# A first pass that loads two tiles in one transfer of 16896 bytes per partition, into four double buffers

## The chip, the cores and the metric

The kernel runs on one core of a Trainium2 chip. The metric is device microseconds of one execution. An engine is named as in the profile: PE is the matrix engine (PEld its weight loads), DVE the vector engine, ACT the scalar engine, POOL GpSimd, SP the engine that issues most transfers. SPq and ACTq are the instruction queues of SP and ACT, in which transfers (DMA) are issued.

## The reference

The input is x, 16 channels of 2048 x 2048 float32 (268 MB). Four layers follow one another, each `x = x + conv(gn(x))`:

```python
def _gn(v, G=8, eps=1e-5):            # mean and variance over 2 channels x 2048 x 2048
    return ((g - m) / jnp.sqrt(s + eps)).reshape(v.shape)
# conv: the 15 ways to partition {row in, column in, row out, column out};
# each is an einsum of X (itself, its transpose, its diagonal, its row, column and total
# sums, spread over rows, columns, the diagonal or everything) with a 16x16 weight
for i, blocks in enumerate(PARTITIONS):
    Yi = _basis_apply(X, weights[i], blocks, eye_n, ones_n)   # divided by N per summed index
    Y = Yi if Y is None else Y + Yi
return Y + jnp.sum(bias)
```

All of this is linear apart from the normalisation, which needs only a mean and a variance per pair of channels. So the kernel reads x twice: once for its statistics (row sums, column sums, a Gram matrix of the channels, the diagonal), from which small algebra gives one 32x32 channel mixing matrix with its row and column terms for all four layers together, and once to apply them and write the result.

## The kernel before

**First pass, lines 322 to 330, 447 to 452, 456 to 460, 510 to 518 and 661 to 686.** The host lays x out as 272 tiles (`pair_tiles`, `lay_out`): 64 rows by 128 columns of x and of its transpose, 32 channels in all, as 128 partitions of `VW` = 2112 floats, that is 8448 bytes. They lie one after another in DRAM, so that a tile is one contiguous block of 1056 KB. On the chip the tensor `early` holds `V_SLOTS` = 8 such tiles, side by side on each partition; tile t goes to slot t mod 8.

SP runs the loop over the tiles. It issues the first 8 loads at once; after the eighth (t == 7) come the constants and two copies of the diagonal. Before tile t from the ninth on it waits until PE and DVE have finished tile t - 8 (`gram_done` and `summed`, one count per tile). Each slot has its own semaphore `v_in`, which a load raises by 16 as it lands.

For each tile DVE makes one reduction (line 515), the column sums, which POOL adds to `col_sum` (line 449). PE makes 32 matmuls (line 668; the trace counts 64 records for them), which add four tiles, a quad, into four PSUM banks; two quads use the banks in turn, and after each ACT copies them out (line 460) and POOL adds the copy to the Gram matrix and the row sums (lines 365 and 368; in POOL's order, the sum of a quad comes after the column sums of the next one). After tile 4, DVE waits for the constants and the diagonal before it goes on (lines 519 to 523), and PE has a small product of the diagonal between the second and the third quad. PE's quads from the third on are a loop, in which quad q waits until quad q - 2 has been copied out.

**Between the passes.** Once the last tile is in the sums, DVE (lines 540 to 626), PE (691 to 746) and ACT work through the algebra of the four layers in turn, one waiting for the other at nearly every step. SP has by then issued the loads of the first units of the second pass: six and a half units go to `ring_own`, a tensor of their own (lines 333 and 334), and three into `early`, once PE and DVE have finished all tiles (lines 335 to 345); one more may go into `early` only after the algebra.

**Second pass.** x is 256 strips of 128 partitions x 2048 floats and a half strip; two strips are a unit, loaded in one transfer of 2048 KB, 16384 bytes on each partition (line 317), and stored in one (line 494, issued by ACT). PE multiplies each strip by the mixing matrix (line 763), DVE adds the row and column terms back into the buffer (lines 639 and 647). A buffer is loaded again once its store has landed.

Of the kernel before, what the change touches and what calls it, by code (L numbers as in the profile page):

```python
# [8 lines left out]
BLK = 128  # L9
# [11 lines left out]
VW = RANGE // SUB * FOUR  # L21
QUAD = 4
V_SLOTS = 2 * QUAD
# [10 lines left out]
def pair_tiles(n):  # L34


    nb = n // BLK
    out = []
    for J in range(nb // 2 + 1):
        for e in range(2):  # L40
            for first in (J, nb - J) if 0 < J < nb // 2 else (J,):
                out += [(2 * first + e, k) for k in range(first, nb)]
    return out


def quads(n):

    tiles = pair_tiles(n)
    return [list(dict.fromkeys(r for r, _ in tiles[t:t + QUAD])) for t in range(0, len(tiles), QUAD)]


def strips(n):


    groups = n // SUB
    out = [[(0, 0, 0, n)]]
    for q in range(1, groups // 2):
        out.append([(0, q, SUB * q, n - SUB * q), (n - SUB * q, groups - q, n - SUB * q, SUB * q)])
    return out + [[(0, groups // 2, n // 2, n // 2)]]


def lay_out(x):

    n = x.shape[2]
    x = x[0]
    xt = np.ascontiguousarray(x.transpose(0, 2, 1))
    tiles = pair_tiles(n)
    v = np.zeros((len(tiles), BLK, RANGE // SUB, FOUR), np.float32)
    row, col = np.arange(RANGE)[:, None], np.arange(BLK)[None]
    for t, (r, J) in enumerate(tiles):  # L70
        at = PAIR * SUB + COLS * quads(n)[t // QUAD].index(r)
        v[t, :, :, at:at + COLS] = 1.0
        rows, cols = slice(r * RANGE, (r + 1) * RANGE), slice(J * BLK, (J + 1) * BLK)
        for h, a in enumerate((x, xt)):
            blk = a[:, rows, cols]
            if r * RANGE // BLK == J:
                i, j = row + r * RANGE, col + J * BLK
                blk = np.where((i <= j if h == 0 else i < j)[None], blk, np.float32(0))
            blk = blk.reshape(CH, RANGE // SUB, SUB, BLK).transpose(3, 1, 0, 2)
            v[t, :, :, h * CH * SUB:(h + 1) * CH * SUB] = blk.reshape(BLK, RANGE // SUB, CH * SUB)  # L80
    z = np.zeros((len(strips(n)), 2, CH, SUB, n), np.float32)
    for q, strip in enumerate(strips(n)):
        for at, g, j, width in strip:
            for h, a in enumerate((x, xt)):
                z[q, h, :, :, at:at + width] = a[:, SUB * g:SUB * g + SUB, j:j + width]
    return v.reshape(len(tiles), BLK, VW), *as_units(z.reshape(len(strips(n)), BLK, n))


def as_units(z):

    count, _, n = z.shape
    twos = z[:count - 1].reshape(count // 2, 2, BLK, n).transpose(0, 2, 1, 3)
    return np.ascontiguousarray(twos).reshape(count // 2, BLK, 2 * n), np.ascontiguousarray(z[count - 1, :, 0:n // 2])
# [80 lines left out]
def build(nc, n, v, twos, half, dia, dia_pair, weights, biases, const_f32, twos_out, half_out, out_dia, where):  # L174
# [6 lines left out]
    tiles = pair_tiles(n)  # L181
# [11 lines left out]
    with ctx:  # L193
        def sb(name, shape, dt=F32):
            return ctx.enter_context(nc.sbuf_tensor(name, shape, dt))

        def sem(name):
            return ctx.enter_context(nc.semaphore(name))

        Z_OWN = 13  # L200
        early = sb("early", [BLK, V_SLOTS * VW])
        ring_own = sb("ring_own", [BLK, Z_OWN, n])
        vbuf = early[:, :].rearrange("p (s w) -> p s w", s=V_SLOTS)
# [89 lines left out]
            rows = vbuf[:, s].rearrange("p (q e b) -> p q e b", q=RANGE // SUB, b=COLS)  # L293
            return rows[:, k // COLS, 0:width, k % COLS]

        v_in = [sem(f"v_in{s}") for s in range(V_SLOTS)]
        z_in = [sem(f"z_in{s}") for s in range(TWOS + 1)]
        z_out = [sem(f"z_out{s}") for s in range(TWOS + 1)]
        const_in, dia_loaded, weights_in = sem("const_in"), sem("dia_loaded"), sem("weights_in")
# [1 line left out]
        gram_done, summed, sum_added = sem("gram_done"), sem("summed"), sem("sum_added")  # L301
# [11 lines left out]
        @block.sync  # L313
        def _(sp):
            def load(u):
                buf, s, _ = home(u)
                sp.dma_start(buf, half if s == TWOS else twos[units[u][0] // 2]).then_inc(z_in[s], 16)  # L317

            for layer in range(LAYERS):
                sp.dma_start(wt[:, layer], weights[layer].rearrange("k c o -> c k o")).then_inc(weights_in, 16)  # L320
                sp.dma_start(bias_sb[:, layer], biases[layer].rearrange("(z k) -> z k", z=1)).then_inc(weights_in, 16)
            for t in range(len(tiles)):
                if t >= V_SLOTS:
                    sp.wait_ge(gram_done, t - V_SLOTS + 1)
                    sp.wait_ge(summed, t - V_SLOTS + 1)
                sp.dma_start(vbuf[:, t % V_SLOTS], v[t]).then_inc(v_in[t % V_SLOTS], 16)
                if t == V_SLOTS - 1:
                    sp.dma_start(const[:, :], const_f32).then_inc(const_in, 16)
                    sp.dma_start(dia2[:, :, :], dia_pair).then_inc(dia_loaded, 16)
                    sp.dma_start(dia_in[:, :, :], dia).then_inc(dia_loaded, 16)  # L330
            sp.wait_ge(matrices_in, 16 * 13)
            sp.wait_ge(dia_cov_done, 1)
            for u in range(own_twos + 1):
                load(u)
            sp.wait_ge(gram_done, len(tiles))
            sp.wait_ge(summed, len(tiles))
            for u in range(own_twos + 1, len(units)):
                _, s, turn = home(u)
                if turn == 0 and s >= own_twos + reuse:
                    sp.wait_ge(col_term_done, 1)  # L340
                    sp.wait_ge(row_term_done, 1)
                    sp.wait_ge(dia_ready, 1)
                if turn:
                    sp.wait_ge(z_out[s], 16 * turn)
                load(u)
            for s in range(TWOS):
                sp.wait_ge(z_out[s], 16 * len(range(s, half_strip // 2, TWOS)))
            sp.wait_ge(z_out[TWOS], 16)
            sp.wait_ge(dia_out, 16 * 4)
# [151 lines left out]
        def _(dve):  # L501
# [7 lines left out]
            tt = nc.vector.tensor_tensor  # L509
            for t in range(len(tiles)):  # L510
                s = t % V_SLOTS
                dve.wait_ge(v_in[s], 16 * (t // V_SLOTS + 1))
                if t >= sums:
                    dve.wait_ge(sum_added, t - sums + 1)
                nc.vector.tensor_reduce(  # L515
                    part_sum[:, t % sums],
                    vbuf[:, s].rearrange("p (q w) -> p q w", w=FOUR)[:, :, 0:PAIR * SUB].rearrange(
                        "p q (c a) -> p c q a", a=SUB), AX.XY, ALU.add).then_inc(summed, 1)
                if t == 4:
                    dve.wait_ge(const_in, 16)  # L520
                    dve.wait_ge(dia_loaded, 32)
                    tt(dia2s[:, :, :], dia2[:, :, :], c("dia_scale").unsqueeze(1).to_broadcast([BLK, nb, FEATS]),
                       ALU.mult).then_inc(dia_scaled, 1)
                if t == 8:
                    dve.wait_ge(weights_in, 16 * 2 * LAYERS)
                    link(nc.vector.tensor_reduce(beta[:, :], bias_sb[:, :, :], AX.X, ALU.add))
                    link(nc.vector.memset(brow[:, :, :], 0.0))
                    nc.vector.tensor_copy(brow[:, :, 0:4 * CH],
                                          beta[:, :].unsqueeze(2).to_broadcast([1, LAYERS, 4 * CH])).then_inc(beta_done, 1)
                    link(nc.vector.memset(rs[:, :, :], 0.0))  # L530
                    link(nc.vector.memset(normed[:, :], 0.0))
                    nc.vector.memset(normed[96:97, FEATS:FEATS + 1], 1.0)
                    nc.vector.memset(m80[:, :, :], 0.0)
                    link(nc.vector.memset(mean_row[:, :], 0.0))
# [125 lines left out]
        def _(pe):  # L660
            mm = nc.tensor.matmul
            def quad(parity, turn):
                for slot in range(QUAD * parity, QUAD * parity + QUAD):
                    opens, closes = slot % QUAD == 0, slot % QUAD == QUAD - 1
                    pe.wait_ge(v_in[slot], 16 * (turn + 1))
                    for k in range(CHUNKS):
                        m, lane = k // COLS, k % COLS * WIDE
                        last = mm(regions(parity)[lane:lane + WIDE, m // BANK_REGIONS, m % BANK_REGIONS],  # L668
                                  chunk(slot, k, WIDE), chunk(slot, k, WIDE + MARKS),
                                  start=opens and m % BANK_REGIONS == 0,  # L670
                                  stop=closes and m % BANK_REGIONS == BANK_REGIONS - 1)
                    last.then_inc(gram_done, 1)
# [75 lines left out]
            for p, (u, k, q) in enumerate(order):  # L748
                buf, first = strip_buf(u, k), 4 * (p % 2)
                _, s, turn = home(u)  # L750
# [58 lines left out]
```

## Time and profile before

| | us |
|---|---|
| median of 3 runs | 2044.98 (2041.34 to 2045.75) |
| the profiled execution, its time | 2041.38 |
| its span, first to last instruction | 2039.1 |
| PE / DVE / POOL / ACT busy | 1630.1 / 1333.5 / 256.5 / 79.1 |
| moved by DMA | 834.80 MB in 78957 packets, 409 GB/s over the span |
| first pass: the last tile's load issued, and landed | at 695.92, 18.1 later |
| second pass: first matmul with the mixer | at 805.8 |

Times within the trace are microseconds from the start of the span. Views of the trace that are used below: the 40 equal slices of the span (a digit is a busy share in tenths, PEclk the clock granted to PE); the chain of waits that ended last; the waits by engine; busy times, granted clock, DMA share and GB/s of a stretch; the instructions in order of time; and the time from a transfer's issue to its landing.

### The profile page before, as it was taken

To read this page: it belongs to the slowest core of one execution; us is meant where nothing else is said; L and a number is where in the kernel's file an instruction comes from. 1 tells how busy PE (TensorE), PEld (TensorE's weight loads), DVE (VectorE), ACT (ScalarE), POOL (GpSimd) and SP (SyncE) were. 2 spreads that over 40 slices of the span, in tenths; PEclk is the share of its full clock that TensorE was granted. 3 is DMA by queue.
4 is the path that set the end of the run, shared out by engine and by line. 5 is a ranking of instruction groups with operands and counts; after the bars stand their busy time and mean duration, and the time that the engine had idled before them with its cause. 6 is when DMAs were issued, how large, how long until landed. Compare 5 with 4: busy or idle time off the path is not lost.

```text
span 2039.1 us, 43249 instructions
## 1 busy us (share of the span) xinstructions
PE 1630.1 (80%) x19730; PEld 999.9 (49%) x19730; DVE 1333.5 (65%) x1285; ACT 79.1 (4%) x80; POOL 256.5 (13%) x488
## 2 busy tenths in 40 slices
PE   6888888888888858999887778777877777778773
PEld 6877777777777753344333333333333333333331
DVE  5988888888888832677555555555555555555553
ACT  0111111001111100000000000000000000000000
POOL 6333333333333310000000000000000000000000
PEclk9999999999999965999999999999999999999987
DMA  9999999999999980899999999999999999999998
GB/s 376 416 415 414 422 422 423 422 422 422 422 422 422 424 352 0 331 431 431 430 431 431 431 431 431 431 431 431 431 431 430 431 431 430 431 431 431 431 430 372
DMA packets 78957, 834.80 MB, mean 409 GB/s; under 512 B 10617, under 2 KB 10745, under 8 KB 11321
## 3 DMA queue, kind: packets, MB, share of 16 engines
q1 hardware_dynamic: 59208, 564.76, 65.9%
q10 hardware_dynamic: 19696, 269.40, 30.9%
q8 instruction: 27, 0.44, 0.1%
q14 instruction: 26, 0.20, 0.0%
HBM read 564.73 MB, written 269.09 MB: 409 GB/s over the span
## 4 chain that ended last, share of the span: by engine, by line
another core or an unknown queue 47%; DMA 33%; PE 10%; DVE 6%; SPq 2%; issue 1%; POOL 0%; ACT 0%; DVEq 0%; POOLq 0%
DMA early<-pairs 28%; PE ps L763 6%; DVE ring_own L515 5%; DMA out<-early 2%; SPq L317 2%; DMA early<-strip_in 1%; DMA dia_in<-dia 1%; PE ps L742 0%; PE ps L744 0%; PE ps L738 0%; PE ps L698 0%; PE ps L692 0%; PE ps L770 0%; POOL gram_all L365 0%
## 5 line engine op out<-in xcount | busy, mean ns | idle before, releaser
L763 PE MATMUL ps<-ring_own,mixer 128*128 128x512 f32 x1252 | 592.9, 631 | 137.5 <-DMA ring_own<-strip_in 126.8
L668 PE MATMUL ps<-early 128*64 128x66 f32 x17408 | 590.6, 224 | 121.6 <-DMA early<-pairs 114.3
L515 DVE TENSOR_REDUCE ring_own<-early 128x32 f32<-128x2048 f32 x272 | 619.9, 2285 | 84.0 <-DMA early<-pairs 83.6
L668 PEld LDWEIGHTS ps<-early 128*64 128x64 f32 x17408 | 554.6, 138 | 157.4 <-DMA early<-pairs 130.3
L639 DVE SCALAR_TENSOR_TENSOR ring_own<-ps,row_sum,stage 128x512 f32<-128x512 f32 (+3 forms) x233 | 301.6, 1295 | 331.4 <-PE ps L763 331.4
L763 PEld LDWEIGHTS ps<-ring_own,mixer 128*128 128x128 f32 x1252 | 247.0, 202 | 484.6 <-issue 468.9
L763 PE MATMUL ps<-early,mixer 128*128 128x512 f32 x800 | 374.5, 625 | 89.6 <-DMA early<-strip_in 79.0
L639 DVE SCALAR_TENSOR_TENSOR early<-ps,row_sum,stage 128x1024 f32<-128x1024 f32 (+2 forms) x152 | 192.6, 1267 | 197.2 <-PE ps L763 197.2
L763 PEld LDWEIGHTS ps<-early,mixer 128*128 128x128 f32 x800 | 156.2, 200 | 307.5 <-issue 296.1
L365 POOL TENSOR_TENSOR gram_all<-gram_all,stage 128x1024 f32<-128x1024 f32 x68 | 150.5, 2213 | 0.3
L647 DVE SCALAR_TENSOR_TENSOR ring_own<-ps,row_sum,stage 128x488 f32<-128x488 f32 (+43 forms) x308 | 133.4, 475 | 0.0
L449 POOL TENSOR_TENSOR col_sum<-col_sum,ring_own 128x32 f32<-128x32 f32 x272 | 68.8, 253 | 457.3 <-DVE ring_own L515 456.6
L460 ACT ACTIVATE stage<-ps 128x1056 f32<-128x1056 f32 x68 | 71.7, 1054 | 640.4 <-PE ps L668 640.4
L647 DVE SCALAR_TENSOR_TENSOR early<-ps,row_sum,stage 128x464 f32<-128x464 f32 (+49 forms) x200 | 86.6, 475 | 0.0
L368 POOL TENSOR_TENSOR row_sum<-row_sum,stage 128x16 f32<-128x16 f32 x80 | 18.0, 232 | 0.0
L381 POOL TENSOR_TENSOR ring_own<-ring_own 16x64 f32<-16x64 f32 x51 | 17.2, 338 | 4.0
L692 PE MATMUL ps<-const,early 128*128 128x32 f32 x32 | 7.0, 401 | 7.9 <-DVE early L540 7.9
L692 PEld LDWEIGHTS ps<-const,early 128*128 128x128 f32 x32 | 6.9, 332 | 8.0 <-issue 8.0
L742 PE MATMUL ps<-early,coef_t 80*128 80x512 f32 x8 | 8.3, 1142 | 0.0
L744 PE MATMUL ps<-gram_all 1*128 1x512 f32 x8 | 8.3, 1136 | 0.0
L738 PE MATMUL ps<-early,stage 80*128 80x512 f32 x8 | 7.5, 1099 | 0.8 <-DVE mixer L621 0.8
L722 PE MATMUL ps<-normed,step_m 96*96 96x80 f32 x8 | 2.4, 408 | 7.2 <-DVE normed L598 7.2
(137 smaller groups left out, 133.9 us busy)
## 6 DMA issues: line engine op xcount, KB each, us to landing
early<-pairs SPq DMA_DIRECT2D x272, 1056.0 KB, 18.1
ring_own<-strip_in SPq DMA_DIRECT2D x78, 2048.0 KB, 23.3
out<-ring_own ACTq DMA_DIRECT2D x78, 2048.0 KB, 63.1
early<-strip_in SPq DMA_DIRECT2D x50, 2048.0 KB, 23.3
out<-early ACTq DMA_DIRECT2D x50, 2048.0 KB, 63.4
const<-const_f SPq DMA_DIRECT2D x1, 781.0 KB, 22.2
ring_own<-dia_pair SPq DMA_DIRECT2D x1, 640.0 KB, 21.8
ring_own<-half_in SPq DMA_DIRECT2D x1, 512.0 KB, 36.5
```

What stands on the lines that cost most here:

```text
L317: sp.dma_start(buf, half if s == TWOS else twos[units[u][0] // 2]).then_inc(z_in[s], 16)
L365: nc.gpsimd.tensor_tensor(gram_all[:, :, 0:WIDE], gram_all[:, :, 0:WIDE], got[:, :, 0:WIDE], ALU.add)
L368: last = nc.gpsimd.tensor_tensor(rows, rows, got[:, :, WIDE + k], ALU.add)
L381: link(nc.gpsimd.tensor_tensor(dst, a, b, op))
L449: nc.gpsimd.tensor_tensor(col_sum[:, J], col_sum[:, J], part_sum[:, t % sums], ALU.add).then_inc(sum_added, 1)
L460: nc.scalar.activation(stage[:, q % 2].rearrange("p (b m) w -> p b m w", m=BANK_REGIONS), regions(q), ACT.Copy).then_inc(gram_staged, 1)
L515: nc.vector.tensor_reduce(part_sum[:, t % sums], vbuf[:, s].rearrange("p (q w) -> p q w", w=FOUR)[:, :, 0:PAIR * SUB].rearrange("p q (c a) ...
L639: ins = nc.vector.scalar_tensor_tensor(buf[:, at + done:at + done + wide * BANK].rearrange("p (b w) -> p b w", b=wide), acc[:, b:b + wide] ...
L647: ins = nc.vector.scalar_tensor_tensor(buf[:, at + done:at + done + piece], acc[:, b, off:off + piece], row_term[:, g:g + 1], col_term[:, ...
L668: last = mm(regions(parity)[lane:lane + WIDE, m // BANK_REGIONS, m % BANK_REGIONS], chunk(slot, k, WIDE), chunk(slot, k, WIDE + MARKS), st ...
L692: last = mm(ps[:, 0, b * PAIR:(b + 1) * PAIR], spread[:, b * per_block:(b + 1) * per_block].rearrange("p g a -> p (g a)"), c("pair"), star ...
L763: last = mm(ps[:, first + at // BANK, 0:piece], mixer[:, :, :].rearrange("p c a -> p (c a)"), buf[:, at:at + piece], start=True, stop=True)
```

## The change

The host puts the tiles t and t + 1 (t even) side by side on each partition: 136 blocks of 128 x 16896 bytes in place of 272 of 128 x 8448. SP issues one transfer for two tiles, into two neighbouring slots, and before the fifth and each later one it waits until PE and DVE have finished both tiles that lie there. Four semaphores, one for a pair of slots, stand in place of eight. DVE still waits before each tile, on the semaphore of the pair; PE waits only before the first tile of a pair. The constants are issued after the fourth double transfer, so behind the same 8 tiles. Nothing changes in what DVE, PE, ACT and POOL compute, in which order, or in the second pass. The bytes are the same.

```diff
-    return v.reshape(len(tiles), BLK, VW), *as_units(z.reshape(len(strips(n)), BLK, n))
+    v = v.reshape(len(tiles) // 2, 2, BLK, VW).transpose(0, 2, 1, 3)
+    return np.ascontiguousarray(v).reshape(len(tiles) // 2, BLK, 2 * VW), *as_units(z.reshape(len(strips(n)), BLK, n))
...
-        v_in = [sem(f"v_in{s}") for s in range(V_SLOTS)]
+        v_in = [sem(f"v_in{s}") for s in range(V_SLOTS // 2)]
...
-            for t in range(len(tiles)):
+            for t in range(0, len(tiles), 2):
+                s = t % V_SLOTS
                 if t >= V_SLOTS:
-                    sp.wait_ge(gram_done, t - V_SLOTS + 1)
-                    sp.wait_ge(summed, t - V_SLOTS + 1)
-                sp.dma_start(vbuf[:, t % V_SLOTS], v[t]).then_inc(v_in[t % V_SLOTS], 16)
-                if t == V_SLOTS - 1:
+                    sp.wait_ge(gram_done, t - V_SLOTS + 2)
+                    sp.wait_ge(summed, t - V_SLOTS + 2)
+                sp.dma_start(early[:, s * VW:(s + 2) * VW], v[t // 2]).then_inc(v_in[s // 2], 16)
+                if t == V_SLOTS - 2:
...
-                dve.wait_ge(v_in[s], 16 * (t // V_SLOTS + 1))
+                dve.wait_ge(v_in[s // 2], 16 * (t // V_SLOTS + 1))
...
-                    pe.wait_ge(v_in[slot], 16 * (turn + 1))
+                    if slot % 2 == 0:
+                        pe.wait_ge(v_in[slot // 2], 16 * (turn + 1))
```

## Rows read from the trace of the kernel before

**Rows 1.** The span in 40 slices: granted PE clock, mean share of 16 DMA engines.

```profile
PEclk9999999999999965999999999999999999999987
DMA  9999999999999980899999999999999999999998
```

**Rows 2.** Waits: engine, line, what it waited for: total us, times, longest.

```profile
PE ps L668 <- DMA early<-pairs: 114.3, 253, 8.8
...
DVE ring_own L515 <- DMA early<-pairs: 83.6, 248, 8.8
...
SPq L325 <- DVE ring_own L515: 578.0, 264, 12.6
```

**Rows 3.** DMA queues: packets, MB, share; issues: count, KB each, us to landing.

```profile
q1 hardware_dynamic: 59208, 564.76, 65.9%
q10 hardware_dynamic: 19696, 269.40, 30.9%
...
early<-pairs SPq DMA_DIRECT2D x272, 1056.0 KB, 18.1
```

**Rows 4.** Stretches: busy PE, PEld, DVE, ACT, POOL (count), clock, DMA share, GB/s.

```profile
200.00:712.00 512.00, 430.72 (x12736) 403.33 (x12731) 454.67 (x200) 52.69 (x50) 167.90 (x309) 1.00 1.01 422
45.00:50.00 5.00, 3.25 (x105) 3.11 (x101) 5.00 (x3) 1.05 (x1) 0.51 (x2) 1.00 1.00 414
50.00:55.00 5.00, 4.70 (x102) 4.70 (x104) 5.00 (x3) 0.00 (x0) 2.81 (x4) 0.66 1.01 421
1000.00:1900.00 900.00, 703.36 (x1477) 290.83 (x1476) 492.24 (x655) 0.00 (x0) 0.00 (x0) 0.94 1.01 431
```

**Rows 5.** The chain of waits, in order of time: start, us, what.

```profile
199.06 18.09 DMA early<-pairs
...
363.41 18.78 DMA early<-pairs
...
693.35 18.11 DMA early<-pairs
...
1107.28 9.44 another core or an unknown queue
...
1909.80 9.42 another core or an unknown queue
```

**Rows 6.** First-pass loads (line 326): all 272, to landing.

```profile
DMA to landing us min/median/max: 5.1/18.1/22.7
```

**Rows 7.** SP's queue after the last tile; the last strip load, to landing.

```profile
695.92 0.33 SPq L326 DMA_DIRECT2D early<-pairs  x1
...
L317 SPq DMA_DIRECT2D early<-strip_in x1: 434/434/434, 717.3 to 717.3; - x1
...
DMA to landing us min/median/max: 42.1/42.1/42.1
```

**Rows 8.** Instructions in order of time: start, us, engine, line, what, [idle before].

```profile
32.03 1.49 DVE L522 TENSOR_TENSOR ring_own<-ring_own,const 128x1280 f32<-128x1280 f32 x1 [9.30 <-DMA dia_in<-dia]
...
44.14 41.76 DVE L515 TENSOR_REDUCE ring_own<-early 128x32 f32<-128x2048 f32 x19
...
44.08 4.17 PE L668 MATMUL ps<-early 128*64 128x66 f32 x128 [1.31 <-issue]
50.30 5.67 PE L668 MATMUL ps<-early 128*64 128x66 f32 x128 [2.05 <-issue]
```

**Rows 9.** The same, from the last tile to the first step of the algebra.

```profile
714.05 2.29 DVE L515 TENSOR_REDUCE ring_own<-early 128x32 f32<-128x2048 f32 x1 [0.28 <-DMA early<-pairs]
...
714.07 2.19 PE L668 MATMUL ps<-early 128*64 128x66 f32 x64 [0.40 <-DMA early<-pairs]
...
716.41 0.25 POOL L449 TENSOR_TENSOR col_sum<-col_sum,ring_own 128x32 f32<-128x32 f32 x1 [2.31 <-DVE ring_own L515]
...
721.67 2.29 DVE L540 TENSOR_TENSOR early<-row_sum,const 128x2048 f32<-128x2048 f32 x1 [5.34 <-POOL row_sum L368]
```

## The prediction

> **What bounds the kernel now.** I read the slices of the whole span first [rows 1]. DMA shows a 9 in every slice but three in the middle and the last: in both passes the 16 DMA engines are full nearly everywhere, and only the algebra between the passes leaves them idle. The stretch from 200 to 712 says the same more closely [rows 4]: DMA share 1.01 (the view counts about half a per cent too much), while PE is busy 430.7 of 512 us and DVE 454.7. The waits come next [rows 2]: both PE and DVE wait for tiles to land, some 250 times, about 0.4 us each on average, so they are faster than the transfers. SP's long wait for DVE (578.0 us) looks like the bound and isn't one: it is the wait for a free slot. What decides is how much work lies in the queue when SP is let go. A lone first tile lands 5.1 us after its issue, the usual one after 18.1 [rows 6], so the usual tile stands behind seven others (7 x 2.57 = 18.0).
>
> Next I take rates from distances between equal events, which the windows blur. In the chain of waits a load that was 8 tiles further on starts at 199.06 and 24 rows later at 693.35, one row per 8 tiles [rows 5]: 494.29 / 192 = 2.574 us per tile of 1.0813 MB, 420.0 GB/s. In the second pass (82 units from 1107.28 to 1909.80 [rows 5]) a unit takes 9.787 us for a load and a store of 2.097 MB each: 428.6 GB/s. Strips alone, without stores: the last tile lands at 695.92 + 18.1 = 714.0, the last of nine and a quarter strip loads behind it at 717.3 + 42.1 = 759.4 [rows 7], so 45.4 / 9.25 = 4.908 us each, 427.3 GB/s. Rows of 16384 bytes move 1.7 to 2.0% faster than rows of 8448, with stores or without.
>
> **How much of that is packets.** The packet counts settle what a row is [rows 3]. The ACT queue has 19696: 128 stores x (128 rows + 16) = 18432, and the small ones give the rest. So a row of 16384 bytes is one packet, and each DMA adds one short packet per engine, its semaphore. SP's queue: 272 x 144 = 39168 for the tiles and 20040 for the others, 59208. Every DMA, tile or strip, is thus 8 rows and one short packet on each engine. Taking time per DMA = a + bytes per engine x b: tile 67584 B in 2.574 us, strip unit 131072 B in 4.908. b = 2.334 / 63488 = 36.8 ns per KB of 1000 bytes, a = 2.574 - 2.484 = 0.090 us, about 10 ns per packet.
>
> **The change, part by part.**
>
> 1. Loads. 136 DMAs of 8 x 16896 bytes per engine: 0.090 + 135168 B x 36.76 ns/KB = 5.059 us, against 2 x 2.5744 = 5.149. Saved, a once for each pair, 0.090 x 136 = 12.2 us, all on the path, because DMA is full from the first tile to the last (a byte that comes earlier brings all later ones forward). The packets fall by 136 x 144 = 19584, to 59373 in all. Ends for this term: with the second pass's unit in place of the lone strips (9.787 / 2 = 4.893) a is 0.106 and the saving 14.4 us. Without the irregular tiles (one chain row in six is 18.78 in place of 18.1 [rows 5]; a tile without them is 2.562) a is 0.065 and the saving 8.8. Outer ends: nothing, if the row is not what costs; and 24.5 us, if a vanishes at 16896 bytes (135168 B alone are 4.969 us). I take 12.2, the value from loads without stores.
>
> 2. The first pass's end. The last two tiles now land together. Before, DVE started the last tile at 714.05 and the algebra followed from there: reduction 2.29, then POOL's sums, then line 540 at 721.67 [rows 9]. Now DVE has two reductions after the landing, and the first costs 2.20 when it follows without a gap (41.76 / 19 [rows 8]): +2.2 us. PE's 2 x 2.19 ends sooner than DVE's 4.5, and ACT's copy lies beside POOL's work. Nothing hides this: in the algebra DMA runs dry in any case (the 0 in [rows 1]), and the second pass starts when the algebra ends. The algebra itself is unchanged, its PE at the low clock as before.
>
> 3. Waits and issues. SP issues 136 fewer DMAs at 0.33 us each [rows 7]; SP is never late, so nothing. PE loses 136 waits on semaphores that are up: nothing; ends -0.1 and 0.
>
> 4. Depth of the buffers: what the coarser release costs. Slots come free in twos, 4.5 us after a landing. At that moment the next pair has 0.5 us to go and two stand behind it: 10.6 us of queued transfers. Before it was 18.1 - 2.57 = 15.5. What must be covered is a lone load's overhead, 5.1 - 2.57 = 2.5 us. It is covered four times over, so 0 us; landing should take 4 x 5.059 - 4.6 = 15.6 us in place of 18.1. The thinnest place is the start. DVE stands until 32.03 for the diagonal [rows 8], so the slots of tiles 4 and 5 come free together at about 35.7. Behind the constants, which land as DVE resumes, there are then tiles 8 to 11, good until 32 + 10.1 = 42.1. Tiles 6 and 7 free theirs at 40.1, 8 and 9 (with DVE's extra work after tile 8, about 1.9 us before 44.14) at 46.4, when the queue reaches to 52. At least 5 us are left, more later. If that cover were gone, each such release would cost what it is late, 2 to 3 us once or twice.
>
> Sum: 2041.38 - 12.2 + 2.2 = 2031.4 us for an execution like the profiled one (span 2029.1). That execution is 3.6 below the median of the runs shown (2044.98), near their lowest; the same difference on the median gives 2035.0. Between the two I say 2033.0.
>
> **A rule weighed against the trace.** The Trainium skill (page "DMA: Bandwidth & Descriptors", section "Bandwidth", under why small descriptors are slow) says that a packet costs a fixed 3 cycles or so beside one beat per 32 bytes. With the beat at 32 x 36.76 / 1000 = 1.18 ns that is 3.5 ns where the rows give 10; by it the change would save 1224 packets per engine x 3.5 ns = 4.3 us, 2.1 after the tail. The same page's section "Rules for kernel authors" asks for 1 MiB per DMA for full bandwidth, which a tile already is; it speaks against any gain. The rows speak for one, since strips of 2 MiB do go faster.
>
> **Rivals.**
>
> A. The row isn't what costs. Tiles and strips could differ for another reason, such as instruction fetches or the irregular 18.78 landings, which would stay; or a packet costs a third of what I give it. Saving 0 to 4.3, tail +2.2: time 2039.3 to 2043.6, no change that can be told. For it: the irregular landings alone account for 0.5 of the 2%. Against it: two independent strip rates agree. The same end comes if a row above 16384 bytes, which no DMA here has, is cut into 16384 + 512: packets fall only by the semaphores' 136 x 16 (to 76781), the saving is 136 x 10 ns, and the time 2042.2.
>
> B. Slower: PE falls to 1.2 GHz inside the first pass. Two tiles in a row are 4.3 us of matmuls, and the gap grows from 0.4 to 5.06 - 4.3 = 0.75 us. At the low clock a pair takes 8.6 us of PE, more than the 5.06 of its transfer, and its release would come later than the 10.6 us queue less the 2.5 can bear for long: 3.6 us lost for every such pair. It cancels the gain from 3 pairs (10.0 / 3.6) and shows as slower from 4 (14.1 / 3.6), some 35 us at the low clock beyond what the queue absorbs. If 10% of the pass were so, 8 pairs, +28 us: 2060. For it: after an idle PE of 2.05 us at 50.30 the clock shows 0.66 [rows 4, 8], and the second pass, with its longer gaps, has 0.94. Against it: an idle of 1.31 us (44.08) left it at 1.00 [rows 4, 8], and 0.75 is shorter. The start may have one dip more (PE waits for the diagonal after tile 7), which ends within a few us, and the queue holds 5.
>
> C. More than forecast: the fixed part shrinks with the longer row, or 8448-byte rows suffer otherwise. Up to 24.5 saved less 2.2: 2019.1.
>
> **Numbers.** Forecast 0.71, with its own range 2028 to 2038; A 0.15; B 0.07; C 0.07. Less than 0.2% (4.1 us) is about what a measurement of this kernel can't tell from no change. Faster: forecast and C, with a rounding down for the spread of the runs, 0.77. Same: A, 0.15. Slower: B and an unforeseen loss in the transfers, 0.08. The range reaches to C's middle and A's end, 2024 to 2045.
>
> **What the profile after would show.** Right: 136 first-pass loads of 2112 KB, about 59370 packets, 15 to 16 us to landing; equal marks in the chain 20.2 us apart for 8 tiles where they were 20.5 to 20.6; the stretch 200 to 700 at 429 to 431 GB/s by the window view, which gave 422; the last pair landing near 701.8; line 540 at 711.7 (9.9 after that landing, where it was 7.7). Then all as before, 10.0 earlier. Wrong: some 76800 packets; the rate at 422 (A); a PEclk below 9 in the first pass's slices beyond 50 us, or a DMA digit below 9 there (B); a landing under 12 us, which would mean that the queue runs nearly dry.

## The result, and the profile after

| | before | after |
|---|---|---|
| median us | 2044.98 (2041.34 to 2045.89, 7 runs) | 2037.58 (2034.81 to 2038.35, 7 runs) |
| ratio | | 0.9966, 95% interval 0.9954 to 0.9977 |
| profiled execution: time, span | 2041.38, 2039.1 | 2037.44, 2035.2 |
| packets | 78957 | 59370 |
| last landing of the first pass | 714.0 | 704.4 |
| first step of the algebra (line 540, now 542) | 721.67 | 714.25 |
| from there to the end of the span | 1317.4 | 1321.0 |

The change makes the kernel faster by 7.4 us (0.34%). The forecast was 2033.0, with its own range of 2028 to 2038; the time lies 4.6 us above the forecast and 0.4 us inside the range.

Slices of the span after, the SP queue's packets, the loads, and the stretch from 200 to 700, which answer to [rows 1, 3, 4]:

```profile
PEclk9999999999999955899999999999999989999997
DMA  9999999999999960899999999999999999999998
...
q1 hardware_dynamic: 39624, 564.75, 65.4%
...
early<-pairs SPq DMA_DIRECT2D x136, 2112.0 KB, 15.6
...
200.00:700.00 500.00, 405.47 (x12639) 392.23 (x12636) 442.33 (x199) 52.56 (x50) 168.15 (x307) 1.00 1.01 428
```

The rate rose from 422 to 428 in the view's counting (forecast 429 to 431), landing takes 15.6 us as worked out, PE's clock is 1.00 in this stretch and the packets are 59370. The chain of waits gives the exact distances. Two neighbouring rows of before, each 8 tiles behind the last:

```profile
281.41 18.11 DMA early<-pairs
301.90 18.13 DMA early<-pairs
```

and after, as [rows 5]:

```profile
202.81 15.64 DMA early<-pairs
...
283.58 15.59 DMA early<-pairs
...
303.75 15.60 DMA early<-pairs
...
688.80 15.61 DMA early<-pairs
```

A mark is the distance between two such rows, 8 tiles. From 202.81 to 688.80 are 24 marks, 20.25 us each with the irregular ones (forecast 20.24), where they were 20.60. An undisturbed mark is 20.17 to 20.20, where it was 20.5. The end of the pass, as [rows 9] (start, us, engine, line):

```profile
704.44 4.48 DVE L517 TENSOR_REDUCE ring_own<-early 128x32 f32<-128x2048 f32 x2 [0.57 <-DMA early<-pairs]
...
714.25 2.29 DVE L542 TENSOR_TENSOR early<-row_sum,const 128x2048 f32<-128x2048 f32 x1 [5.33 <-POOL row_sum L370]
```

Both tiles of the last pair are reduced after one landing, and the algebra starts 9.8 us behind it (forecast 9.9; before, 7.6 from 714.05 to 721.67). The landing was forecast near 701.8 and the algebra at 711.7; both came 2.6 us later.

The last row of the table is a trap. The two spans differ by 3.9 us, the medians by 7.4. The part behind the first pass has two lengths that come whatever the kernel: 1317.4 in the profile of before, 1317.9 in one variant below (e_two_rows), and 1320.1 to 1321.6 in ten profiles, those of four kernels with rows of 8448 bytes or fewer among them. The profile of before was a short one, that of after a long one. Line 540 against line 542 shows the change itself: 7.4 us, as do the medians.

### The profile page after: what moved, and what is told of

It reads as the page before. It is cut to its first block, busy times and chain, and to the rows that moved or that the text cites. A ratio compares the mean times of both kernels' runs of the same rounds, so it can differ in the third digit from the quotient of the medians.

```text
span 2035.2 us, 42981 instructions
## 1 busy us (share of the span) xinstructions
PE 1607.9 (79%) x19730; PEld 990.7 (49%) x19730; DVE 1322.1 (65%) x1285; ACT 78.9 (4%) x80; POOL 258.7 (13%) x488
## 2 busy tenths in 40 slices
DMA packets 59370, 834.78 MB, mean 410 GB/s; under 512 B 8440, under 2 KB 8568, under 8 KB 9144
## 3 DMA queue, kind: packets, MB, share of 16 engines
q1 hardware_dynamic: 39624, 564.75, 65.4%
## 4 chain that ended last, share of the span: by engine, by line
another core or an unknown queue 47%; DMA 28%; PE 12%; DVE 5%; issue 4%; SPq 2%; POOL 0%; ACT 0%; DVEq 0%; POOLq 0%
DMA early<-pairs 24%; PE ps L766 6%; DVE ring_own L517 4%; PE ps L671 3%; DMA out<-ring_own 2%; SPq L318 2%; DMA early<-strip_in 1%; PE ps L745 0%; PE ps L747 0%; PE ps L741 0%; PE ps L701 0%; PE ps L695 0%; PE ps L773 0%; PE ps L772 0%
## 5 line engine op out<-in xcount | busy, mean ns | idle before, releaser
L671 PE MATMUL ps<-early 128*64 128x66 f32 x17408 | 560.1, 223 | 146.0 <-DMA early<-pairs 129.2
L517 DVE TENSOR_REDUCE ring_own<-early 128x32 f32<-128x2048 f32 x272 | 608.5, 2281 | 90.5 <-DMA early<-pairs 90.4
L671 PEld LDWEIGHTS ps<-early 128*64 128x64 f32 x17408 | 542.5, 138 | 163.5 <-DMA early<-pairs 112.6
L766 PE MATMUL ps<-early,mixer 128*128 128x512 f32 x800 | 379.3, 631 | 88.4 <-DMA early<-strip_in 66.9
## 6 DMA issues: line engine op xcount, KB each, us to landing
early<-pairs SPq DMA_DIRECT2D x136, 2112.0 KB, 15.6
```

The costliest lines, as they stand in the source:

```text
L517: nc.vector.tensor_reduce(part_sum[:, t % sums], vbuf[:, s].rearrange("p (q w) -> p q w", w=FOUR)[:, :, 0:PAIR * SUB].rearrange("p q (c a) ...
L766: last = mm(ps[:, first + at // BANK, 0:piece], mixer[:, :, :].rearrange("p c a -> p (c a)"), buf[:, at:at + piece], start=True, stop=True)
```

## Experiments

All are compared by the median, and by two places in the trace: the distance of undisturbed marks, and the start of the algebra. Each ratio is to the kernel before as it ran beside that kernel, with medians of 2043.32 to 2045.05; so medians of different rows can be off by a microsecond or two against each other. The algebra's start of one profile isn't exact either: three profiles of the same schedule and packets (changed, c_after, x_after_shift) have 714.25, 714.52 and 715.94.

| kernel | bytes of a packet | DMAs of the pass | mark | algebra at | median (runs) | ratio to before, 95% |
|---|---|---|---|---|---|---|
| before | 8448 | 272 | 20.5 | 721.67 | 2044.98 (7) | |
| changed | 16896 | 136 | 20.2 | 714.25 | 2037.58 (7) | 0.9954 to 0.9977 |
| c_after | 16896 | 136 | 20.2 | 714.52 | 2036.83 (5) | 0.9950 to 0.9977 |
| x_src | 8448 | 272 | 20.5 | 721.17 | 2044.19 (11) | 0.9986 to 1.0004 |
| x_after_shift | 16896 | 136 | 20.2 | 715.94 | 2037.58 (5) | 0.9946 to 0.9974 |
| e_half_rows | 4224 | 272 | 20.5 | 721.68 | 2043.85 (10) | 0.9987 to 1.0006 |
| e_two_rows | 8448 | 136 | 20.5 | 723.66 | 2046.74 (11) | 1.0000 to 1.0018 |
| e_gap2 | 8448 | 136 | 20.5 | 724.08 | 2046.34 (10) | 1.0002 to 1.0021 |
| e_gap4 | 4224 | 136 | 20.5 | 723.54 | 2047.03 (8) | 1.0005 to 1.0025 |
| e_mat_a | 16896 | 136 | 20.2 | 712.78 | 2036.05 (5) | 0.9940 to 0.9967 |
| e_last_single | 16896 | 137 | 20.2 | 718.90 | 2038.67 (10) | 0.9964 to 0.9983 |
| e_combo | 16896 | 136 | 20.2 | 710.99 | 2033.70 (5) | 0.9940 to 0.9967 |
| e_quads | 33792 | 68 | 22.5 (mean) | 796.59 | 2121.85 (2) | 1.0357 to 1.0395 |

**The changed kernel again** (c_after, no edit).

> The changed kernel again, for a second profile of it. Theory 1 (the gain is made in the first pass and nothing in the second pass depends on the change): the first step of the algebra starts 7.4 us earlier than in the kernel before's profile (714.25 against 721.67), within 0.3, and what lies between that and the end differs from profile to profile by some 3 us either way; the median is 7 to 8 us below the kernel before. Theory 2 (the change also makes the second pass slower, as the first pair of profiles has it: gain 7.4 at the algebra, 3.9 at the end): the end is again only about 4 us earlier than 2039.1.

Algebra at 714.52, rest 1321.2, median 7.6 below the kernel before that ran beside it. Theory 1 stands: a second pass of the changed kernel isn't slower; kernels with the old rows (x_src 1321.3, e_half_rows 1321.5) have the long rest too.

**What of a transfer is cheaper: the DMA, the packet, or its place?** First the changed kernel's schedule with the rows of before (e_two_rows):

```diff
-    v = v.reshape(len(tiles) // 2, 2, BLK, VW).transpose(0, 2, 1, 3)
-    return np.ascontiguousarray(v).reshape(len(tiles) // 2, BLK, 2 * VW), *as_units(z.reshape(len(strips(n)), BLK, n))
+    return v.reshape(len(tiles) // 2, 2, BLK, VW), *as_units(z.reshape(len(strips(n)), BLK, n))
...
-                sp.dma_start(early[:, s * VW:(s + 2) * VW], v[t // 2]).then_inc(v_in[s // 2], 16)
+                sp.dma_start(vbuf[:, s:s + 2], v[t // 2].rearrange("s p w -> p s w")).then_inc(v_in[s // 2], 16)
```

> The changed kernel's schedule (136 DMAs, release and semaphore by pairs), but each partition's 16896 bytes come as two rows of 8448, as the tiles lay before. Packets per pair and engine: 17, where the changed kernel has 9 and the kernel before 18. Theory P (each packet costs about 10 ns): the rate stays at 420 GB/s, saving 136 x 10 ns = 1.4 us, tail +2.2, so about 1 us slower than the kernel before (2046) and 8 slower than the changed one. Theory D (the cost is one of the DMA or its semaphore, not of the rows): as the changed kernel, 2037.6, marks 20.18 us apart for 8 tiles.

The gain is gone (an undisturbed mark is 20.5 again) and the tail stays, 2046.74: the number of DMAs and semaphores is not what costs. Then the kernel before with rows cut in two (e_half_rows: v laid out as two planes of 128 x 1056 floats per tile, loaded by `v[t].rearrange("h p w -> p h w")`):

> The kernel before with each tile's rows cut in two, 4224 bytes each: 272 DMAs as before, 17 packets per engine and DMA in place of 9. Theory P: 272 x 8 x 10 ns = 21.8 us slower than before, 2066.8, marks 20.5 + 0.64 = 21.1 us apart. Theory D: no change, 2045. In between, the cost per packet can be read off: excess / 2176.

This one went against me. There are 34816 more packets and no more time. So a fixed 10 ns for each packet, my model, is wrong, although it had given the right rate for 16896 bytes. Two more kernels ask whether the start of a row decides: x_src lays the rows of before 8704 bytes apart in DRAM, so that each starts at a multiple of 512, and x_after_shift lets the changed kernel's start 256 bytes past a multiple of 512 on both sides (`early[:, 64 + s * VW:64 + (s + 2) * VW]` from `v[t // 2][:, 64:64 + 2 * VW]`).

> The kernel before, its rows of 8448 bytes laid 8704 apart in DRAM, so that every row starts at a multiple of 512 bytes there (before, every second one starts 256 past one). SBUF side, row length, DMAs and packets unchanged. Theory A (half of the 8448-byte rows pay for their start in DRAM): marks of 8 tiles fall from 20.50 towards 20.18, time 2035 to 2040. Theory L (the length of the row, or what is left of it over whole blocks of 512, is what counts) and theory S (the start in SBUF counts): no change, 2044.

> The changed kernel with its rows of 16896 bytes starting 256 bytes past a multiple of 512, in DRAM (rows 17408 apart) and in SBUF. Theories A and S: each row now pays as the misaligned ones before, marks 20.18 rise to about 20.3 to 20.5, time 2040 to 2044. Theory L: no change, 2037.

Neither moves: marks 20.5 and 20.2, medians as their parents'. The start is out. (That x_after_shift's algebra starts 1.4 to 1.7 us behind the other two comes from the first 90 us, point 4 below, and from a few more irregular marks, not from the pace.) The last pair keeps everything of the changed kernel but the packet, by a gap of 256 bytes in DRAM after every k-th part of a row (k = 2, and 4 in e_gap4):

```diff
-    return np.ascontiguousarray(v).reshape(len(tiles) // 2, BLK, 2 * VW), *as_units(z.reshape(len(strips(n)), BLK, n))
+    pieces = np.zeros((len(tiles) // 2, BLK, 2, 2112 + 64), np.float32)
+    pieces[:, :, :, 0:2112] = v.reshape(len(tiles) // 2, BLK, 2, 2112)
+    return pieces, *as_units(z.reshape(len(strips(n)), BLK, n))
...
-                sp.dma_start(early[:, s * VW:(s + 2) * VW], v[t // 2]).then_inc(v_in[s // 2], 16)
+                sp.dma_start(early[:, s * VW:(s + 2) * VW].rearrange("p (k w) -> p k w", k=2),
+                             v[t // 2][:, :, 0:2112]).then_inc(v_in[s // 2], 16)
```

> The changed kernel, but a partition's 16896 bytes lie in DRAM as two pieces of 8448 with a gap of 256 bytes, so that a packet carries 8448 bytes while the place in DRAM, the destination, the order and the number of DMAs stay. Packets of a pair: 17 per engine in place of 9. Theory B (what counts is how many bytes one packet moves): as the kernel before, marks of 8 tiles 20.5 apart (two pieces a megabyte apart gave that), time 2045 to 2047 with the tail. Theory N (what counts is that the two tiles are neighbours in DRAM): as the changed kernel, 20.18 and 2037.

> The same with four pieces of 4224 bytes and gaps of 256: 33 packets per pair and engine. A fixed cost of about 9 ns per packet would give 8 x 9 x 4 x 2 = 0.6 us more per mark than two pieces, 21.1, and 2060. Rows of 4224 bytes in an order of their own gave 20.51 instead; if that holds, the gain from 4224 to 8448 is nil and only the step to 16896 pays: marks 20.5, time 2046.

Queue and chain of e_gap2:

```profile
q1 hardware_dynamic: 57032, 564.75, 65.8%
...
657.38 15.90 DMA early<-pairs
...
677.85 15.91 DMA early<-pairs
...
698.34 15.90 DMA early<-pairs
```

and of e_gap4:

```profile
q1 hardware_dynamic: 91848, 564.75, 66.2%
...
656.80 15.91 DMA early<-pairs
...
677.28 15.93 DMA early<-pairs
...
697.79 15.92 DMA early<-pairs
```

20.47 and 20.49 us per mark with 57032 packets, 20.48 and 20.51 with 91848, 20.2 with 39624. What the gain needs is packets of 16896 bytes; between 4224 and 8448 the shorter packet costs nothing more. Why the step lies there no run shows, nor whether the strips with their 16384 bytes owe their rate to the same.

**Where the missing gain went** (e_mat_a). The chain fixes the pair of tiles 78 and 79: before it was complete at 219.74, in the changed kernel at 218.47, in its second profile at 217.94. That is 1.3 and 1.8 us of gain for 40 pairs, where 3.6 were due; the other 96 pairs brought 8.3 and 7.5 (8.6 due). In that time ACT issues 12 small transfers of the layer matrices, 4 rows of 384 bytes for each of 16 partitions; 10 of them fall between 88 and 194 us. One line makes them rows of 1536:

```diff
-        place = [place_buf[:, m * wsize:(m + 1) * wsize].rearrange("p (l r o) -> p l r o", l=LAYERS, r=6)
+        place = [place_buf[:, m * wsize:(m + 1) * wsize].rearrange("p (r l o) -> p l r o", l=LAYERS, r=6)
```

> The changed kernel with the layer matrices laid out on GpSimd's side so that each of the 12 small transfers between quads 5 and 16 has one row of 1536 bytes per partition in place of four of 384. In that stretch the profiles give 10.5 us for two pairs against 10.12 elsewhere, 0.37 per small transfer (0.25 in the kernel before). Theory M (their short packets cost it): 3 to 3.5 us less from 88 to 193 us, the 24th to 34th landing at the steady pace, time 2034. Rival (the cost is per small DMA or comes from GpSimd, DVE or ACT): under 1 us, 2037.

Two equal places 40 tiles apart (DVE, in order of time), before:

```profile
88.72 2.29 DVE L515 TENSOR_REDUCE ring_own<-early 128x32 f32<-128x2048 f32 x1 [0.27 <-DMA early<-pairs]
...
193.90 2.29 DVE L515 TENSOR_REDUCE ring_own<-early 128x32 f32<-128x2048 f32 x1 [0.27 <-DMA early<-pairs]
```

in the changed kernel:

```profile
87.98 4.48 DVE L517 TENSOR_REDUCE ring_own<-early 128x32 f32<-128x2048 f32 x2 [1.02 <-DMA early<-pairs]
...
192.88 4.48 DVE L517 TENSOR_REDUCE ring_own<-early 128x32 f32<-128x2048 f32 x2 [0.53 <-DMA early<-pairs]
```

and with the longer matrix rows:

```profile
87.88 4.48 DVE L517 TENSOR_REDUCE ring_own<-early 128x32 f32<-128x2048 f32 x2 [0.90 <-DMA early<-pairs]
...
191.25 4.48 DVE L517 TENSOR_REDUCE ring_own<-early 128x32 f32<-128x2048 f32 x2 [0.58 <-DMA early<-pairs]
```

The stretch takes 104.9 us (104.7 in the second profile) and 103.4 with the edit; before, the same 40 tiles took 105.2. At the undisturbed pace it would be 101.0 after and 102.5 before. So the stretch is 2.7 us over its pace before, 3.9 with the long packets, and 2.4 when the small transfers have fewer rows. These 20 pairs owed a gain of 1.8 us and kept 0.3. Half of theory M: 1.5 us of the 3 to 3.5 expected. The profiles spread a little: four with long packets and the old matrix rows have 104.5 to 105.1 here, the two with the edit (e_combo is the other) 103.4 and 103.6, so 1.3 us on the mean. That the number of short rows counts is shown; what makes up the 2.4 us that remain isn't.

The time to landing of such a small transfer shows the other side of the meeting. Each fence is one row of the view of issues; the kernels stand in the order before, changed, e_mat_a, e_gap4, e_quads:

```profile
step_m<-ring_own ACTq DMA_DIRECT2D x6, 24.0 KB, 6.6
```

```profile
step_m<-ring_own ACTq DMA_DIRECT2D x6, 24.0 KB, 7.9
```

```profile
step_m<-ring_own ACTq DMA_DIRECT2D x6, 24.0 KB, 5.9
```

```profile
step_m<-ring_own ACTq DMA_DIRECT2D x6, 24.0 KB, 5.4
```

```profile
step_m<-ring_own ACTq DMA_DIRECT2D x6, 24.0 KB, 10.5
```

With the big queue's packets at 4224, 8448, 16896 and 33792 bytes a small transfer lands after 5.4, 6.6, 7.9 and 10.5 us. That fits engines that serve their queues in turn, a whole packet at a time: each short row then waits for a longer packet of the other queue. The Trainium skill says so too (page "DMA: Bandwidth & Descriptors", section "Queues, rings and completion order": round-robin between queues at packet granularity), and the four landing times rise as it would have them. An estimate of the size: an engine has 4 of the 64 short rows, and at the 36.8 ns per KB worked out from the strips a packet of 8448 bytes takes 0.31 us, so the steps should be 0.6, 1.2 and 2.5 us; measured 1.2, 1.3 and 2.6. One row in place of four beside packets of 16896 bytes should save 1.9; measured 2.0 (7.9 to 5.9). Only the first step doesn't fit. Why the big queue in turn loses 0.39 us per small transfer beside long packets and 0.27 beside short ones, this doesn't say, and no run shows.

**The tail** (e_last_single: the last pair as two single loads with a semaphore of its own for the last tile, and PE's last turn of the loop written out).

```diff
+                if t == len(tiles) - 2:
+                    sp.dma_start(vbuf[:, s], v[t // 2][:, 0:VW]).then_inc(v_in[s // 2], 16)
+                    sp.dma_start(vbuf[:, s + 1], v[t // 2][:, VW:2 * VW]).then_inc(v_last, 16)
+                    continue
...
-            with pe.Fori(1, len(spans) // 2) as turn:
+            end = len(spans) // 2 - 1
+            with pe.Fori(1, end) as turn:
...
+            pe.wait_ge(gram_staged, 2 * end)
+            quad(1, end, True)
```

> The changed kernel with its last double transfer issued as two single ones (own semaphore for the last tile; PE's last turn of the loop is written out for the extra wait). Theory T (the tail of two reductions after one landing costs 2.2 us): the algebra starts 7.7 us after the last landing in place of 9.8, time 2035.4, 2.2 below the changed kernel. Rival: the tail is hidden behind POOL's and ACT's work, no change, 2037.6.

Slower instead, 2038.67. PE in order of time, from the last pair but one:

```profile
706.62 5.67 PE L680 MATMUL ps<-early 128*64 128x66 f32 x128 [2.01 <-issue]
712.82 2.36 PE L680 MATMUL ps<-early 128*64 128x66 f32 x69 [0.53 <-issue]
```

The written-out turn stops PE about every 128 records (2.01 us, and a granted clock of 0.83 from 706 to 716), as it does in the first tiles of every kernel here and never inside the loop once it has run; instructions that had to be fetched are the likely reason, which was not tested by itself. The last tile had landed at 707.5 and PE ended at 715.2. So this run says nothing of the tail; the stops lose what it should have won, with the algebra 11.4 us behind the landing. The rest of its 718.90 is older: this profile is of the longest of its ten executions (2042.36), and the last landing is 3.1 us behind the changed kernel's, mostly lost before tile 30 (point 4 below).

**The tail hidden another way** (e_combo: e_mat_a, and GpSimd's order changed).

```diff
             for t, (r, J) in enumerate(tiles):
+                if t == len(tiles) - 2:
+                    add_quad(len(spans) - 2)
...
-                if t % QUAD == QUAD - 1 and t > QUAD:
+                if t % QUAD == QUAD - 1 and QUAD < t < len(tiles) - 1:
```

> The changed kernel with the layer matrices in rows of 1536 bytes, and GpSimd adding the last quad but one before it waits for the last two tiles instead of after them (2.1 + 0.25 us of its work, now beside the landing and DVE's two reductions). The last quad's sum then follows PE's 4.3 us and ACT's 1.05: the algebra should start 8.0 us after the last landing in place of 9.8. Expected 2034.3: 1.8 below the kernel with the matrices alone (2036.05), some 10 below the kernel before. Rival (PE or the clock then sets the algebra's start): no more than 0.5 below it.

```profile
703.16 4.48 DVE L519 TENSOR_REDUCE ring_own<-early 128x32 f32<-128x2048 f32 x2 [0.57 <-DMA early<-pairs]
...
710.99 2.29 DVE L544 TENSOR_TENSOR early<-row_sum,const 128x2048 f32<-128x2048 f32 x1 [3.35 <-POOL row_sum L370]
```

```profile
707.72 0.25 POOL L453 TENSOR_TENSOR col_sum<-col_sum,ring_own 128x32 f32<-128x32 f32 x1 [1.95 <-DVE ring_own L519]
708.43 2.17 POOL L367 TENSOR_TENSOR gram_all<-gram_all,stage 128x1024 f32<-128x1024 f32 x1 [0.46 <-ACT stage L464]
```

The algebra starts 7.8 us after the landing in place of 9.8, and 0.46 us of that GpSimd waits for ACT's copy of the last quad. Against e_mat_a's profile the algebra starts 1.8 us earlier (710.99 and 712.78). 2033.70 us is 9.6 below the kernel before that ran beside it, a ratio of 0.9954 (0.9940 to 0.9967). Next to the changed kernel (7.4 to 7.6 below its own) the intervals overlap, as they do with e_mat_a (9.0 below); that it is the fastest of all rests on the algebra's start, 3.3 and 3.5 us ahead of the two profiles of the changed kernel.

**How much cover the release needs** (e_quads: four tiles in one transfer, two buffers; all the 2s of the change become 4s).

> Four tiles in one transfer (33792 bytes per partition) into two buffers of four. It tests what cover the release needs. A buffer comes free 9.0 us after its landing (3 x 2.20 + 2.29 and the wait), the other buffer's transfer then has 10.12 - 9.0 = 1.1 us to go, and a lone load needs 2.5 to 2.8 us before its bytes flow and after they do. If that is the rule, DMA idles 1.4 to 1.7 us per transfer, 68 times: +95 to +115, and +4.4 for a tail of four reductions: 2137 to 2157, DMA share in the first pass about 0.87. If the overhead of a queued load is less than that of the first one, near 2045.

```profile
200.00:700.00 500.00, 390.41 (x11427) 385.27 (x11426) 394.31 (x178) 46.23 (x44) 149.85 (x277) 0.91 0.94 384
```

```profile
DVE ring_own L517 <- DMA early<-pairs: 183.1, 68, 16.2
```

2121.85, 84 us above the changed kernel, and DMA share 0.94. Over 25 marks (205.94 to 769.22 in the chain) a mark takes 22.53 us against 20.25, so 1.14 us are lost per transfer, 78 in all, and 4.4 by the tail. But two causes are in this. PE's clock is down to 0.91, in a kernel where PE stands still for about 3 us per quad, and a quad that can take 8 us takes up to 10.6. So in 30 of the 66 waits it is PE, not DVE, that lets SP go:

```profile
SPq L328 <- PE ps L671: 35.4, 30, 2.8
...
311.28 10.60 PE L671 MATMUL ps<-early 128*64 128x66 f32 x256 [3.75 <-DMA early<-pairs]
```

Where DVE was the last, several times in a row, the cover shows alone:

```profile
366.52 8.87 DVE L517 TENSOR_REDUCE ring_own<-early 128x32 f32<-128x2048 f32 x4 [1.62 <-DMA early<-pairs]
377.20 8.87 DVE L517 TENSOR_REDUCE ring_own<-early 128x32 f32<-128x2048 f32 x4 [1.81 <-DMA early<-pairs]
387.90 8.87 DVE L517 TENSOR_REDUCE ring_own<-early 128x32 f32<-128x2048 f32 x4 [1.84 <-DMA early<-pairs]
```

The landings are 10.7 us apart there in place of 10.12, and some 1.7 us of transfer were still queued at the next issue. So a queued load needs about 2.3 us ahead of its bytes (an estimate, 1.7 + 0.6), near the 2.5 of the prediction. The loss is 0.6 us per transfer and not 1.4 to 1.7 because each late landing also gives the next release more cover. That makes some 40 us in all; the other 40 or so come with PE's late releases, which the expectation didn't have. The changed kernel, with 10.6 us in the queue, is far from that edge in its steady part.

## Why the prediction was right, and where it was off

1. Loads: forecast 12.2 us earlier, measured 9.6 at the last landing (9.3 in the second profile). From tile 80 on the forecast holds: 8.3 and 7.5 of 8.6 us. The mis-sized term is that all 136 pairs save 0.090. The first 40 saved 1.3 and 1.8 in place of 3.6. Of what is missing, 1.5 and 1.3 us are missing between tiles 30 and 69, where the small transfers of ACT, which I had left where they were at no cost, meet the longer packets; e_mat_a and e_combo get 1.3 of it back by their row count alone. Another 0.6 and 0.3 are missing before tile 30 (point 4). The slower stretch was in the trace of before: the tiles between 88 and 194 landed 0.27 us late per small transfer. I had seen it only as a rate.
2. The split of time into a per-DMA and a per-packet part was a fit of two points. It gave the right number at 16896 bytes and a wrong one (+21.8 us) at 4224. So the right number for 16896 came by luck as far as the model goes: the strips, from which it was fitted, had rows about as long as the new ones. The rule of the Trainium skill weighed ahead of the result (page "DMA: Bandwidth & Descriptors", section "Bandwidth": some 3 cycles per packet) doesn't fit either: from 91848 to 57032 packets a mark changes by some 0.02 us, where 64 packets per engine at the prediction's estimate of 3.5 ns would be 0.22, and from 57032 to 39624 a mark falls by 0.3 us, 9 ns for each of the 32 packets per engine that it loses.
3. Tail: +2.2 forecast, 9.8 - 7.6 = 2.2 measured. That it was on the path e_combo shows, where GpSimd's work moved beside it and the algebra came 2.0 us sooner after the landing.
4. Depth: no cost in the steady part, landing 15.6 as worked out. The start is not free, though the prediction put it at nothing. In the first 90 us PE falls behind by its stops at 128 records, and SP waits for PE 16.6 us in all (4.9 before). From 60 to 75 us the transfers move 413 GB/s in the changed kernel's profile, 429 in its second, 408 in x_after_shift and 376 in e_last_single (420 before), where SP waits for PE 14.0, 24.9 and 23.7 us in the last three. Against 429 that is 0.6, 0, 0.7 and 1.9 us lost (an estimate from the rates), about what the prediction gave for a cover that is gone once.
5. Rival A's outcome (no gain) is what e_two_rows and e_gap2 show when the packet stays short. Its case of a row cut at 16384 bytes is refuted by the packet count, 59370. Rival B (PE's clock) did not happen: 1.00 from 10 to 700 us. In the second profile the clock is 0.89 from 60 to 75, and the transfers keep their 429 GB/s. Rival C: no.
6. Between the algebra's start and the first strip 0.4 to 0.8 us were lost in both profiles of the changed kernel (799.23 - 714.25 = 85.0, and 84.6, against 84.2 before); x_src, with the old rows, has 85.0 too, so it is not the change.
7. The base: of the 4.6 us between forecast and measurement only 2.6 are the loads. The other 2.0 come from saying 2033.0, halfway between 2031.4 (from the profiled execution) and 2035.0 (from the median). What is compared is the median, and 2035.0 + 2.6 is 2037.6. The profiled execution was low because it was one of the short ones. That the time lies inside the range, by 0.4 us, is partly luck.
8. A reading that was off without harm: the usual landing time of 18.1 us isn't seven tiles of 2.57. SP issues a load when the tile of 8 before it has been reduced, 2.3 us after that one's landing, so it is eight tiles less the reduction: 20.6 - 2.3 = 18.3.

## What to carry to other kernels

When a queue is full, look at what a byte costs in the stretches that already have the form you mean to introduce, and believe the rate rather than the model behind it. Here longer packets made every small transfer on the same engines land later, and the stretch where they met kept hardly any of the gain: count the short transfers before you multiply a saving by all of its loads. When you test how much must be queued, look at who lets the issuing engine go; in e_quads it was PE in nearly half of the cases. And a coarser transfer lengthens what follows the last landing; look there for work of another engine that can go ahead of it, and compare two profiles at a mark inside, since their ends can differ for reasons of their own.

## What was not expected

Packets of 4224 and of 8448 bytes give the same rate (marks of 20.5 us, 422 GB/s in the view), and 16896 gives 1.5% more. A small transfer's landing grows from 5.4 to 10.5 us with the length of the packets beside it. The part behind the first pass takes 1317.4 to 1317.9 or 1320.1 to 1321.6 us, whatever the kernel; in the short form PE's 68 records of the first strips take 30.9 us, in the long one 31.2 to 32.1 at a granted clock that dips a little earlier. What decides between the two stays open.
